# Sampled-softmax loss: one fp32 product of 65 rows with the bias in the gathered rows, all masks by tensor-scalar on VectorE, and a semaphore per gather

## What is computed

```python
def reference(r_movie_id, r_target_movie_id, L0_rec_sampled_ids, L0_rec_front_emb, L0_rec_after_emb, L0_rec_after_bias):
...
        inputs = front_emb[movie_id[:, 0]]
        labels = target_movie_id[:, 0]
        true_w = after_emb[labels]
        true_b = after_bias[labels]
        samp_w = after_emb[sampled_ids]
        samp_b = after_bias[sampled_ids]
        true_logits = jnp.sum(inputs * true_w, axis=-1) + true_b
        sampled_logits = jnp.einsum('bd,sd->bs', inputs, samp_w) + samp_b
        true_logits = true_logits - jnp.log(_log_uniform_expected_count(labels, NUM_SAMPLED, VOCAB))
        sampled_logits = sampled_logits - jnp.log(_log_uniform_expected_count(sampled_ids, NUM_SAMPLED, VOCAB))[None, :]
        hits = sampled_ids[None, :] == labels[:, None]
        sampled_logits = jnp.where(hits, sampled_logits + NEG_INF, sampled_logits)
        logits = jnp.concatenate([true_logits[:, None], sampled_logits], axis=1)
        loss = jax.nn.logsumexp(logits, axis=1) - logits[:, 0]
```

## Time and profile before

| what | value |
|---|---|
| median of 3 runs | 83.03 us (82.94 to 88.99) |
| span of the profiled execution | 79.0 us |
| instructions | 638 |
| PE busy | 42.1 us (53%) |
| PEld busy | 27.1 us (34%) |
| DVE busy | 47.2 us (60%) |
| ACT busy | 46.3 us (59%) |
| POOL busy | 42.3 us (54%) |
| mean granted TensorE clock | 0.838 |

### The profile page before, as it was taken

One profiled execution on the slowest core, in us unless ns is written; L12 is line 12 of the kernel. 1 busy time (PEld: TensorE's weight loads), 2 busy tenths in 40 slices (PEclk: granted clock), 3 DMA queues, 4 the chain that ended last, 5 costly groups with the idle time before them and its releaser, 6 DMA issues.

```text
span 79.0 us, 638 instructions
## 1 busy us (share of the span) xinstructions
PE 42.1 (53%) x139; PEld 27.1 (34%) x139; DVE 47.2 (60%) x148; ACT 46.3 (59%) x74; POOL 42.3 (54%) x49
## 2 busy tenths in 40 slices
PE   0002599871059969253905605903996796769000
PEld 0002167140047655041604205503573565537000
DVE  0698886780071682648080093622965999998950
ACT  6049996712293092896084023079619895999770
POOL 7578686736868668578776868664680000000000
PEclk9999999998555899999999555555557999999995
DMA  0822121222344575968548689779689100000000
GB/s 7 221 65 33 18 34 17 29 25 17 25 25 18 25 24 18 30 19 21 24 23 30 20 18 29 20 18 33 21 18 30 4 0 8 0 0 0 0 0 4
DMA packets 1715, 1.91 MB, mean 24 GB/s; under 512 B 944, under 2 KB 944, under 8 KB 1712
## 3 DMA queue, kind: packets, MB, share of 16 engines
q0 software_dynamic: 1280, 1.33, 42.7%
q1 hardware_dynamic: 432, 0.55, 2.6%
HBM read 1.87 MB, written 0.01 MB: 24 GB/s over the span
## 4 chain that ended last, share of the span: by engine, by line
issue 26%; PE 21%; DVE 18%; ACT 10%; POOL 9%; another core or an unknown queue 8%; DMA 5%; DVEq 0%
POOL w_rows L219 9%; PE psum L291 8%; DVE psum L512 7%; PE psum L289 7%; ACT psum L339 6%; PE psum L290 5%; DVE masks L404 5%; DMA w_rows<-after,rows 3%; DVE xT L420 2%; DMA id_cols<-ids 2%; DVE lowest L512 1%; ACT masks L311 1%; PE psum L244 1%; DVE prod L521 1%
## 5 line engine op out<-in xcount | busy, mean ns | idle before, releaser
L512 DVE CUSTOM_DVE_ANT_0 psum<-psum,masks 128x1024 f32<-128x1024 f32 x16 | 19.7, 1231 | 16.4 <-PE psum L291 9.1
L289 PE MATMUL psum<-wT_high,xT 128*128 128x512 f32 x32 | 16.4, 511 | 21.3 <-issue 10.5
L339 ACT ACTIVATE psum<-psum,lowest 128x1024 f32<-128x1024 f32 x16 | 17.2, 1077 | 7.7 <-issue 5.2
L219 POOL DMA_INDIRECT t_rows<-after,rows x16 | 16.9, 1058 | 6.5 <-issue 4.7
L219 POOL DMA_INDIRECT x_rows<-front,rows x16 | 15.8, 990 | 6.9 <-issue 4.0
L289 PEld LDWEIGHTS psum<-wT_high,xT 128*128 128x128 f32 x32 | 7.1, 222 | 27.5 <-issue 21.2
L291 PE MATMUL psum<-b_parts,ones 128*128 128x512 f32 x32 | 14.8, 463 | 0.0
L290 PE MATMUL psum<-wT_low,xT 128*128 128x512 f32 x32 | 14.7, 460 | 0.0
L311 ACT ACTIVATE masks<-sample_ids,neg_label 128x1024 f32<-128x1024 int32 x9 | 10.3, 1140 | 3.1 <-DMA sample_ids<-sample_row 3.1
L334 ACT ACTIVATE xT<-psum 64x256 fp32r<-64x256 f32 (+1 forms) x9 | 3.0, 349 | 13.7 <-remote 7.4
L317 ACT ACTIVATE masks<-masks,ln_big 128x1024 f32<-128x1024 f32 x9 | 10.3, 1142 | 0.1
(11 more groups left out here) (78 smaller groups left out, 33.2 us busy)
## 6 DMA issues: line engine op xcount, KB each, us to landing
sample_ids<-sample_row SPq DMA_DIRECT2D x1, 512.0 KB, 3.9
x_rows<-front,rows POOLq DMA_INDIRECT x16
t_rows<-after,rows POOLq DMA_INDIRECT x16
w_rows<-after,rows POOLq DMA_INDIRECT x8
id_cols<-ids SPq DMA_DIRECT2D x1, 20.0 KB, 1.7
out<-loss SPq DMA_DIRECT2D x1, 8.0 KB, 1.4
```

What stands on the lines that cost most here:

```text
L219: return pool.indirect_dma_start(dst, None, table, bass.IndirectOffsetOnAxis(ap=rows[:, col:col + 1], axis=0))
L289: nc.tensor.matmul(o, x, wT_high[:, part], start=True, stop=False)
L339: nc.scalar.activation(logits(t), logits(t), ACT.Exp, bias=lowest[:, 0, t:t + 1], scale=-1.0, accum_out=sums[:, t:t + 1]).then_inc(exp_ok, 1)
L512: V.tensor_tensor_reduce(out=logits(t), in0=logits(t), in1=masks[:, t, :], scale=1.0, scalar=3e38, op0=ALU.add, op1=ALU.min, accum_out=low ...
```

## The change

TensorE's product of a tile becomes one fp32 product over 65 rows in each bank (`score`, new L222): `wT` and `xT` are plain fp32 with 65 rows. The 65th row of `wT` is the bias minus the log of the count, which VectorE writes into the gathered rows ahead of the transposes (`bias_w`); that of `xT` is minus one, from the ones in the 65th column of `x_rows`. High and low parts, the bias's split, its transposes and its product go, with `raise_w`'s second copy and all of `lower_w` and `lower_x`. ScalarE makes no masks. VectorE makes all 16 by one tensor-scalar operation with the label as a per-partition scalar and 1e9 as a constant; 11 stand ahead of the first reduction (EARLY_MASKS), the others behind those of tiles 0, 2, 4, 6 and 8. Each group of x and each target tile has a semaphore of its own, and GpSimd waits for no gather. The dots stand later (9 behind tiles 11 to 15, 7 at the end), and the end of the computation is another formula with one more step on ScalarE.

```diff
-T_SEMS = 4
...
-ACT_MASKS = (0, 2, 4, 6, 8, 10, 12, 13, 15)
+EARLY_MASKS = 11
...
-        wT_high = sb("wT_high", [P, SAMPLES], f32r)
-        wT_low = sb("wT_low", [P, SAMPLES], f32r)
-        xT = sb("xT", [P, BATCH], f32r)
-        b_cols = sb("b_cols", [P, SAMPLE_TILES])
-        b_split = sb("b_split", [P, SAMPLE_TILES, 2], f32r)
-        b_parts = sb("b_parts", [P, SAMPLES], f32r)
-        ones = sb("ones", [P, P], f32r)
+        wT = sb("wT", [AUG, SAMPLES])
+        xT = sb("xT", [AUG, BATCH])
...
-            return sum(16 * (b - a) for a, b in X_GROUPS[g % 2:g + 1:2])
...
+        def x_arrived(g):
+            a, b = X_GROUPS[g]
+            return 16 * (b - a)
...
-        x_in = [sem(f"x_in{k}") for k in range(2)]
-        t_in = [sem(f"t_in{k}") for k in range(T_SEMS)]
+        x_in = [sem(f"x_in{g}") for g in range(len(X_GROUPS))]
+        t_in = [sem(f"t_in{t}") for t in range(TILES)]
...
-                if g >= 2:
-                    pool.wait_ge(x_in[g % 2], x_arrived(g - 2))
                 for t in range(*X_GROUPS[g]):
-                    gather(x_rows[:, t, 0:EMBED], front, MOV + t).then_inc(x_in[g % 2], 16)
+                    gather(x_rows[:, t, 0:EMBED], front, MOV + t).then_inc(x_in[g], 16)
             for t in range(TILES):
-                if t >= T_SEMS:
-                    pool.wait_ge(t_in[t % T_SEMS], 16 * (t // T_SEMS))
-                gather(t_rows[:, t, :], after, LAB + t).then_inc(t_in[t % T_SEMS], 16)
+                gather(t_rows[:, t, :], after, LAB + t).then_inc(t_in[t], 16)
...
-                pe.wait_ge(w_in[q], 32)
+                pe.wait_ge(w_bias_ok, q + 1)
                 for i in range(2):
-                    m = nc.tensor.transpose(psum[0:EMBED, q, i * P:(i + 1) * P], w_rows[:, 2 * q + i, 0:EMBED],
+                    m = nc.tensor.transpose(psum[0:AUG, q, i * P:(i + 1) * P], w_rows[:, 2 * q + i, :],
                                             ident[:, :])
                 m.then_inc(w_turned, 1)
-            def turn_b(h):
-                for i in range(4):
-                    m = nc.tensor.transpose(psum[0:2, 4 + h, i * P:(i + 1) * P],
-                                            b_split[:, 4 * h + i, :].bitcast(f32), ident[:, :])
-                m.then_inc(b_turned, 1)
...
+            def score(t):
+                if t >= SLOTS:
+                    pe.wait_ge(exp_ok, t - SLOTS + 1)
+                for h in range(2):
+                    m = nc.tensor.matmul(psum[:, 2 * (t % SLOTS) + h, :], xT[:, t * P:(t + 1) * P],
+                                         wT[:, h * BANK:(h + 1) * BANK], start=True, stop=True)
+                m.then_inc(logits_ok, 1)
+            turn_w(0)
+            turn_w(1)
+            keep_busy(2)
+            turn_w(2)
+            keep_busy(5)
+            turn_w(3)
+            keep_busy(2)
             turn_x(0)
             turn_x(1)
-            def score(t):
-                if t >= SLOTS:
-                    pe.wait_ge(exp_ok, t - SLOTS + 1)
-                x = xT[:, t * P:(t + 1) * P]
-                for h in range(2):
-                    part = slice(h * BANK, (h + 1) * BANK)
-                    o = psum[:, 2 * (t % SLOTS) + h, :]
-                    nc.tensor.matmul(o, x, wT_high[:, part], start=True, stop=False)
-                    nc.tensor.matmul(o, x, wT_low[:, part], start=False, stop=False)
-                    m = nc.tensor.matmul(o, ones[:, :], b_parts[:, part], start=False, stop=True)
-                m.then_inc(logits_ok, 1)
-            pe.wait_ge(wT_low_ok, QUARTERS)
-            pe.wait_ge(b_parts_ok, 2)
+            pe.wait_ge(wT_ok, QUARTERS)
...
-            def square(t):
-                nc.scalar.activation(masks[:, t, :], sample_ids[:, :], ACT.Square,
-                                     bias=neg_label[:, t:t + 1], scale=1.0).then_inc(act_square, 1)
-            def hit(t):
-                act.wait_ge(act_square, ACT_MASKS.index(t) + 1)
-                nc.scalar.activation(masks[:, t, :], masks[:, t, :], ACT.Exp, bias=ln_big[:, 0:1],
-                                     scale=-256.0).then_inc(act_mask, 1)
...
+                nc.scalar.copy(wT[:, w_cols(q)], psum[0:AUG, q, 0:2 * P]).then_inc(wT_ok, 1)
+            def negate_x(g):
                 act.wait_ge(x_turned, g + 1)
                 n = x_cols(g).stop - x_cols(g).start
-                nc.scalar.mul(xT[0:EMBED, x_cols(g)], psum[0:EMBED, x_bank(g), 0:n], -1.0).then_inc(x_high_ok, 1)
+                nc.scalar.mul(xT[:, x_cols(g)], psum[0:AUG, x_bank(g), 0:n], -1.0).then_inc(xT_ok, 1)
...
+            for q in range(QUARTERS):
+                copy_w(q)
+            negate_x(0)
+            negate_x(1)
+            negate_x(2)
+            for t in range(TILES):
+                if t % 2 == 0 and 2 <= t < TILES - 2:
+                    negate_x(group_of(t + 2))
+                exps(t)
...
-                V.scalar_tensor_tensor(masks[:, t, :], sample_ids[:, :], label[:, t:t + 1],
-                                       big[:, 0:1].to_broadcast([P, SAMPLES]), ALU.is_equal,
-                                       ALU.mult).then_inc(dve_mask, 1)
-            def lower_w(q):
-                dve.wait_ge(wT_high_ok, q + 1)
-                for half_rows in (slice(0, EMBED), slice(EMBED, P)):
-                    m = V.tensor_tensor(wT_low[half_rows, w_cols(q)], psum[0:EMBED, q, 0:2 * P],
-                                        wT_high[0:EMBED, w_cols(q)].bitcast(f32), ALU.subtract)
-                m.then_inc(wT_low_ok, 1)
-            def lower_x(g):
-                dve.wait_ge(x_high_ok, g + 1)
-                n = x_cols(g).stop - x_cols(g).start
-                V.scalar_tensor_tensor(xT[EMBED:, x_cols(g)], psum[0:EMBED, x_bank(g), 0:n], -1.0,
-                                       xT[0:EMBED, x_cols(g)].bitcast(f32), ALU.mult, ALU.subtract).then_inc(xT_ok, 1)
+                V.tensor_scalar(masks[:, t, :], sample_ids[:, :], label[:, t:t + 1], -NEG_INF, ALU.is_equal,
+                                ALU.mult).then_inc(mask_ok, 1)
+            def bias_w(q):
+                dve.wait_ge(w_in[q], 32)
+                pair = slice(2 * q, 2 * q + 2)
+                V.tensor_tensor(w_rows[:, pair, EMBED], w_rows[:, pair, EMBED], log_count[:, pair],
+                                ALU.subtract).then_inc(w_bias_ok, 1)
...
+            make_mask(0)
             dve.wait_ge(log_count_ok, 1)
-            link(V.tensor_tensor(b_cols[:, :], log_count[:, 0:SAMPLE_TILES], w_rows[:, :, EMBED], ALU.subtract))
-            link(V.tensor_copy(b_split[:, :, 0], b_cols[:, :]))
-            V.tensor_tensor(b_split[:, :, 1], b_cols[:, :], b_split[:, :, 0].bitcast(f32),
-                            ALU.subtract).then_inc(b_split_ok, 1)
-            dve.wait_ge(row_in, 16)
-            make_mask(DVE_MASKS[0])
-            lower_w(3)
-            lower_x(0)
-            lower_x(1)
-            make_mask(DVE_MASKS[1])
+            bias_w(0)
+            bias_w(1)
+            bias_w(2)
+            make_mask(1)
+            make_mask(2)
+            make_mask(3)
+            bias_w(3)
+            for t in range(4, EARLY_MASKS):
+                make_mask(t)
...
-            dots_behind = {8: 1, 9: 2, 10: 2, 11: 2, 12: 2, 13: 2, 14: 4, 15: 1}
+            dots_behind = {11: 1, 12: 2, 13: 2, 14: 2, 15: 2}
...
+                if t % 2 == 0 and EARLY_MASKS + t // 2 < TILES:
+                    make_mask(EARLY_MASKS + t // 2)
...
+            dve.wait_ge(log_sums_ok, 1)
+            link(V.tensor_tensor(base[:, :], log_sums[:, :], lowest[:, :], ALU.subtract))
+            link(V.tensor_tensor(base[:, :], base[:, :], log_count[:, SAMPLE_TILES:], ALU.add))
+            for t in range(dots_done, TILES):
+                dot(t)
             dve.wait_ge(dot_ok, TILES)
-            link(V.tensor_tensor(lowest[:, 1, :], log_count[:, SAMPLE_TILES:], dots[:, :], ALU.subtract))
-            link(V.tensor_tensor(floor[:, :], lowest[:, 0, :], lowest[:, 1, :], ALU.min))
-            V.tensor_tensor(shifted[:, 0, :], floor[:, :], lowest[:, 0, :], ALU.subtract)
-            V.tensor_tensor(shifted[:, 1, :], floor[:, :], lowest[:, 1, :], ALU.subtract).then_inc(shifted_ok, 1)
-            dve.wait_ge(weights_ok, 1)
-            dve.wait_ge(exp_ok, TILES)
-            link(V.tensor_tensor(total[:, :], sums[:, :], weights[:, 0, :], ALU.mult))
-            V.tensor_tensor(total[:, :], total[:, :], weights[:, 1, :], ALU.add).then_inc(total_ok, 1)
-            dve.wait_ge(log_ok, 1)
-            V.tensor_tensor(loss[:, :], log_total[:, :], shifted[:, 1, :], ALU.subtract).then_inc(loss_ok, 1)
+            link(V.tensor_tensor(gap[:, :], base[:, :], dots[:, :], ALU.subtract))
+            V.scalar_tensor_tensor(neg_gap[:, :], gap[:, :], -1.0, gap[:, :], ALU.mult, ALU.min
+                                   ).then_inc(neg_gap_ok, 1)
+            dve.wait_ge(rest_ok, 1)
```

(1 more changed line is left out.)

144 lines of the change are left out of this document (35 added, 109 removed).

## The result

The changed kernel takes 103.37 us (median of 4 runs, 101.43 to 105.0), where the kernel before took 86.01 us (82.94 to 89.42) in the same series: a ratio of 1.225 (1.212 to 1.239). It was forecast at 66.6 us, and a slower kernel with a chance of 0.09. The profiled execution took 101.94 us, with a span of 99.0.

A forecast was written before the change was run, and what follows sets the result against it. Between 22 and 59 us TensorE's late completions while gathers are in flight were taken as the bound. Afterwards gathers done at 56.8, landing 2.5 and the tail gave span 62.6; plus 4.0 that made 66.6 us, range 62 to 77.

The forecast's parts named there:

- Rival 4: TensorE stays at half clock: fp32 product 1.68 us, tile 3.57; 91 us with all 16 tiles so; chance 0.09.
- 0.64 us for a matmul instruction: TensorE's completions while gathers are in flight: 33.4 us over 52 matmul instructions, so three instructions want 1.9 us a tile.
- rival 3: TensorE's completions come late by the signal, 2.8 us each, not by the instruction: 84 us, no change; chance 0.08.
- late completions no longer add a chain of their own: TensorE's completions want 1.9 us a tile, agreeing with its 1.95 of work; before, seven tiles took 4.8 us each.
- The product at full clock: One fp32 product of 512 columns on TensorE: 0.92 us, between bounds of 0.44 and 0.96.
- A tile: TensorE's time for two fp32 products and a pair of transposes: 1.95 us.
- The masks: VectorE's tensor-scalar masks: 0.65 us each, expected 0.55 to 0.80, upper bound the old 1.28.
- First product: TensorE's first product, after x of tile 1 lands: at 20.1 us instead of 22.5.
- Rival 1: VectorE's back-to-back masks lock GpSimd's gathers out for whole runs, losing all 10.4 us: 74 us; chance 0.22.
- all holds together: Time that VectorE's masks hold up GpSimd's gathers: 4.0 us, between 2.6 and 10.4.
- the gathers decide: The chain of gathers ends at 62.6 us, 2 us after TensorE's chain at 60.7, and sets the span.
- the last gather: GpSimd's fortieth gather: done at 56.8 us with holds, 52.8 without; landing 2.5 us later at 59.3.

The follow-up runs named there:

- e7: Changed kernel with each fp32 product made into four one-pass fp32r products over the same 65 rows: 86.1 us, ratio 1.242 to the kernel before.
- e9: Changed kernel with its fp32 products over 128 rows instead of 65, rows doubled and bias left out: 66.08 us, ratio 0.946 to the kernel before.
- e10: Changed kernel with four one-pass products per fp32 product, over 128 rows, bias left out: 65.41 us, ratio 0.945 to the kernel before.
- e12: e6 with VectorE's masks made by the old two-input operation: three runs of 66.77 to 67.02 us, three of 82.9 to 83.08 us.
- e14: e6 with GpSimd's waits between gathers put back: 68.08 us, ratio 0.974 to the kernel before; one of five runs took 87.96 us.
- e5: Changed kernel without edit on another chip: runs of 66.05 and 65.75 us, and four of 85.73 to 87.07 us.
- e15: Changed kernel without edit on one more chip: 84.63 to 87.03 us in all four runs, ratio 1.221 to the kernel before.
- e11: Changed kernel with 20 unread one-pass products over 128 rows ahead of tile 6's transposes: three runs of 65.56 to 66.0 us, three of 72.27 to 72.82.
- e6: Changed kernel with more unread products of ones over 128 rows where TensorE waits at the start: 65.94 us, ratio 0.954 to the kernel before.
- e3: Changed kernel with x and target gathers reading spread rows: 62.72 and 62.43 us in two runs, 83.94 and 84.99 us in two others.

## Why the prediction was wrong

**The step that failed: the clock.** Rival 4 was given 0.09 on the ground that "TensorE is now busy nearly throughout". It was busy throughout and stayed at half, and what the runs tie this to is that the products ran over 65 of the 128 rows. Neither the fp32 form (e7) nor the idle stretches alone (e9, e10) take the clock for good. Over 65 rows the clock fell around waits of which the last took from 0.34 (e7, e12) to 1.32 us (e14), in some executions and not in others (e5's 66.05 us run kept it over 0.76), and 10.00 of 10 us busy didn't bring it back. Rival 4's own numbers held: a product at half clock 1.71 for 1.68, a tile 3.6 for 3.57, the span 60.7 + 26 = 86.7 for e15's 84.7. The Trainium skill (TensorE: Matmul & The Clock Gate, Part 1) has the clock follow how busy TensorE is, so that sustained work would have brought it back; e15 and e7 disagree, with 0.50 in windows that are busy for 10.00 of 10 us. Whether it is the number of rows or how much of the array switches in them wasn't told apart; the 128-row products of e11 multiply nothing but ones, which speaks for the rows without showing it. Of the 36.8 us between forecast and measurement the clock is about 21 (e15 against e6) and TensorE's stalls are 14.6.

**The second step that failed: 0.64 us for a matmul instruction.** From 33.29 us (tile 2's reduction) to 59.96 (tile 5's) four more signals came through, three of products and one of transposes, 6.7 us each, though a tile now has three instructions. The count by instruction is wrong, and rival 3's 2.8 us by signal is too small. They came in TensorE's order, only while gathers were in flight, and only on one chip. More gathers in flight, or passes, could be what counts; the four other chips had nothing to test it on, and the cause is open. That "late completions no longer add a chain of their own" was to bring the greater part of the 16 us forecast, and it brought nothing: TensorE stood for 14.6 us after, where the kernel before had lost 11.7 us of span against the other chips.

**What held.** The product at full clock (e5): 0.86 for 0.92, the upper of the two bounds. A tile: 1.83 for 1.95. The masks: 0.75 us for 0.65, within 0.55 to 0.80. First product at 19.54 for 20.1. Rival 1 fell: gathers started between masks that stood back to back, the longest was stretched to 1.29 us, and all holds together cost at most 2.0 us (last gather done 54.8, against 52.8 without any), where the sum had 4.0 and rival 1 10.4. By the Trainium skill (SBUF — State Buffer, "SBUF: two separate sides"), which was cited for rival 1, a mask in a two-port mode would shut gathers out for its whole length; these rows disagree, unless the masks did not take that mode, which no row shows.

**What held by luck.** With the clock kept and no late completions, the end is the forecast's: the gathers decide, span 63.7 for 62.6 (e6). But the last gather is done 1.8 us earlier than forecast, and lands 5.5 us behind (54.05 + 0.94 to 60.54), not 2.5; and a run takes 2.2 us more than its span (65.9 for 63.7), not 4.0. The three errors nearly cancel in e6's 65.9 us for 66.6. In e3, with spread rows, the last gather lands 1.7 us behind (done 54.81, last dot 56.49), so the landing is the price of reading one row from everywhere.

## What to carry to other kernels

Ask of a product not only how long TensorE is busy with it but over how many of its rows: in this kernel products over half of them could lose the clock around a short wait and run at half for good, so try to fill the waits with products over all rows, or to pad the rows. A delay measured in one profile and divided by a count is not a price; find the count on a second chip or with a second kernel before a sum rests on it. And before a faster engine is bought, look which wait ends last: here one-pass, fp32 and four-product versions all take 65 to 66 us at full clock, for they end when the gathers do.
